# Second attention layer of a graph network on one core: the adjacency mask added by TensorE in PSUM instead of by GpSimd in SBUF

## The reference

```python
v = einsum('bnd,hdo->bhno', x, Wv) + bv
q = einsum('bnd,hdo->bhno', x, Wq) + bq
k = einsum('bnd,hdo->bhno', x, Wk) + bk
scores = einsum('bhno,bhmo->bhnm', q, k) / dk
scores = leaky_relu(scores, 0.2)
scores = scores + (-1e10 * (1.0 - edge_index))[:, None, :, :]
prop = softmax(scores, axis=-1)
feats = einsum('bhnm,bhmo->bhno', prop, v)
out = leaky_relu(mean(feats, axis=1), 0.2)
```

## Time and profile before

| | us |
|---|---|
| median of 3 runs (3578.19 to 3587.32) | 3586.21 |
| the profiled execution | 3591.9 |
| its span | 3590.1 |
| TensorE matmul busy, of the span | 3095.4 |
| VectorE busy | 3037.3 |
| ScalarE busy | 2911.2 |
| GpSimd busy | 1018.2 |

### The profile page before, as it was taken

One profiled execution on the slowest core, in us unless ns is written; L12 is line 12 of the kernel. 1 busy time (PEld: TensorE's weight loads), 2 busy tenths in 40 slices (PEclk: granted clock), 3 DMA queues, 4 the chain that ended last, 5 costly groups with the idle time before them and its releaser, 6 DMA issues. The chain is left out here.

```text
span 3590.1 us, 77844 instructions
## 1 busy us (share of the span) xinstructions
PE 3095.4 (86%) x30972; PEld 1700.4 (47%) x30972; DVE 3037.3 (85%) x4709; ACT 2911.2 (81%) x3505; POOL 1018.2 (28%) x629
## 2 busy tenths in 40 slices
PE   7987998999999969888898898888988988978886
PEld 5664666666666633333333333333333333336665
DVE  6666787778777779999999999999999999975665
ACT  4665777777777759999999999999999999975665
POOL 4433665556656600000000100000001010005764
PEclk9998999999999979999999999999999999987777
DMA  7630000000000000000000000000000000002211
GB/s 244 213 132 20 21 21 21 19 19 21 20 19 21 18 10 10 10 10 10 7 13 10 10 10 10 10 10 7 13 10 10 10 7 13 10 5 69 57 56 33
DMA packets 68394, 111.44 MB, mean 31 GB/s; under 512 B 26452, under 2 KB 26582, under 8 KB 68054
## 3 DMA queue, kind: packets, MB, share of 16 engines
q1 hardware_dynamic: 68054, 106.69, 9.7%
HBM read 86.61 MB, written 18.87 MB: 29 GB/s over the span
## 5 line engine op out<-in xcount | busy, mean ns | idle before, releaser
L1029 ACT ACTIVATE l_scalar_ring<-l_w,l_r 128x1024 f32<-128x1024 f32 x1632 | 1713.1, 1142 | 37.9 <-DVE l_values L1075 27.6
L1143 DVE TENSOR_SCALAR l_vector_ring<-l_w_code,l_r_code 128x2048 f32<-128x2048 f32 x1232 | 1588.9, 1354 | 3.5 <-issue 0.6
L966 PE MATMUL scores<-l_scalar_ring,l_signs 128*32 128x512 f32 x6528 | 794.1, 605 | 90.7 <-ACT l_scalar_ring L1029 90.4
L976 PE MATMUL scores<-l_vector_ring,l_signs_code 128*32 128x512 f16 x9856 | 673.3, 395 | 136.7 <-DVE l_vector_ring L1143 135.8
L242 ACT COPY probs_t<-turned 128x512 f32<-128x512 f32 x576 | 324.3, 586 | 484.9 <-PE turned L201 484.8
L450 POOL TENSOR_TENSOR l_masked<-l_relu,mask 128x1024 f32<-128x1024 f32 x256 | 545.7, 2132 | 419.8 <-ACT l_relu L607 384.6
L976 PEld LDWEIGHTS scores<-l_vector_ring,l_signs_code 128*32 128x32 bf16 x9856 | 243.3, 96 | 589.8 <-DVE l_vector_ring L1143 300.8
L201 PE MATMUL turned<-ident,l_probs 128*128 128x128 f32 x3072 | 440.6, 289 | 12.1 <-issue 7.9
L269 ACT ACTIVATE l_probs<-l_logits,negmax 128x1024 f32<-128x1024 f32 x384 | 443.5, 1155 | 7.6 <-DVE negmax L260 7.6
L966 PEld LDWEIGHTS scores<-l_scalar_ring,l_signs 128*32 128x32 f32 x6528 | 201.0, 110 | 469.6 <-issue 262.9
L260 DVE CUSTOM_DVE_ANT_0 l_logits<-scores,l_masked,l_bound 128x1024 f32<-128x1024 f32 x256 | 328.3, 1282 | 107.3 <-POOL l_masked L450 73.1
(11 more groups left out here) (240 smaller groups left out, 3129.4 us busy)
## 6 DMA issues: line engine op xcount, KB each, us to landing
mask<-masks_kept SPq DMA_DIRECT2D x192, 256.0 KB, 2.6
l_adj<-adj SPq DMA_DIRECT2D x64, 512.0 KB, 5.7
masks_kept<-l_mask_ring SPq DMA_DIRECT2D x64, 256.0 KB, 4.7
x_res<-x SPq DMA_DIRECT2D x8, 256.0 KB, 5.1
out<-x_res SPq DMA_DIRECT2D x8, 256.0 KB, 2.7
l_h<-l_h SPq DMA_DIRECT2D x8, 128.0 KB, 2.9
l_kl<-l_dh SPq DMA_DIRECT2D x32, 2.0 KB, 1.8
l_kl<-l_dl SPq DMA_DIRECT2D x32, 2.0 KB, 1.8
```

Source lines behind the costliest of these rows:

```text
L966: last = nc.tensor.matmul(s.scores[g * ROWS:(g + 1) * ROWS, buf, half, :], signs[:, window], scalar_ring[:, at % SCALAR_RING, g, halves[ha ...
L976: last = nc.tensor.matmul(s.scores[g * ROWS:(g + 1) * ROWS, buf, half, :], signs_code[:, par, g % 2, window], parts(vector_ring[:, at % VE ...
L1029: last = nc.scalar.activation(scalar_ring[:, at % SCALAR_RING, g, :], w[:, par, :], ACT.Relu, bias=r[:, par, column:column + 1])
L1143: last = nc.vector.tensor_scalar(vector_ring[:, at % VECTOR_RING, g:g + 2, :], w_code[:, par, :, :], r_code[:, par, 0, column:column + 1], ...
```

## The change

In the second layer `score` gets one more multiplication for each half: the bf16 mask as the moving operand against a bf16 identity, as the first of the three that add up in the bank. TensorE, not GpSimd, waits for the mask's transfer. The relu of ScalarE now reads masked scores (it gives zero where the mask is), and its buffer is free once VectorE has taken the unit's logits. VectorE's instruction adds the masked scores in PSUM and the relu, and waits for the relu. GpSimd's addition and the tile `masked` go; GpSimd keeps the layer norm's parts. The transfer of the next mask waits for the scores that read the old one. The bf16 identity is one small copy at the layer's start.

```diff
-        sems = make_sems(nc, ctx, layer, ["x_in0", "x_in1", "x_in", "relu_ready", "masked_ready", "bound_ready",
+        sems = make_sems(nc, ctx, layer, ["x_in0", "x_in1", "x_in", "relu_ready", "bound_ready",
...
-        masked = sb("masked", [P, 2, N], F32) if leaky else None
+        ident16 = sb("ident16", [P, P], BF16) if leaky else None
...
                 for m in range(B * NB):
-                    wait(sp, sems["masked_ready"], (m - 1) * H)
+                    wait(sp, sems["scores_ready"], (m - 1) * H)
                     load_mask(sp, s, sems, m, m % 2)
...
-            def mask_relu(pair, i, n, u):
-
-                if n % H == 0:
-                    g.wait_ge(sems[f"mask_in{i}"], 16 * pair + 16)
-                g.wait_ge(sems["relu_ready"], u + 1)
-                wait(g, sems["logits_ready"], STARTS + u - 1)
-                nc.gpsimd.tensor_tensor(masked[:, n % 2, :], relu4[:, n % 2, :], s.mask[:, i, :], ALU.add
-                                        ).then_inc(sems["masked_ready"], 1)
...
-                    if leaky and not (last_graph and n + 3 >= U):
-                        i = ((n + 3) // H) % NB
-                        mask_relu((b + (n + 3) // U) * (NB // 2) + i // 2, i % 2, n + 3, b * U + n + 3)
...
-            if leaky:
-                for u in range(3):
-                    mask_relu(0, 0, u, u)
-            else:
+            if not leaky:
                 layer_norm_centre(g, s, sems, 0, 0)
...
+                if leaky and h == 0:
+                    pe.wait_ge(sems[f"mask_in{i % 2}"], 16 * (b * (NB // 2) + i // 2) + 16)
                 rows = slice(i * P, (i + 1) * P)
                 for half in range(2):
                     cols = slice(half * BANK, (half + 1) * BANK)
                     out = s.scores[:, n % 2, half, :]
-                    nc.tensor.matmul(out, h2[:, par, rows], kh[:, par, h, cols], start=True, stop=False)
+                    if leaky:
+                        nc.tensor.matmul(out, ident16[:], s.mask[:, i % 2, cols], start=True, stop=False)
+                    nc.tensor.matmul(out, h2[:, par, rows], kh[:, par, h, cols], start=not leaky, stop=False)
                     last = nc.tensor.matmul(out, h1[:, par, rows], kl[:, par, h, cols], start=False, stop=True)
...
             def relu(n, u):
                 a.wait_ge(sems["scores_ready"], u + 1)
-                wait(a, sems["masked_ready"], u - 1)
+                wait(a, sems["logits_ready"], STARTS + u - 1)
...
                 if leaky:
-                    v.wait_ge(sems["masked_ready"], u + 1)
-                    masked_max(v, s, sems, scores[n % 2], n % 4, neg_scale, logits[:, n % 2, :], masked[:, n % 2, :])
+                    v.wait_ge(sems["relu_ready"], u + 1)
+                    masked_max(v, s, sems, scores[n % 2], n % 4, neg_scale, logits[:, n % 2, :], relu4[:, n % 2, :])
...
             if leaky:
+                nc.vector.tensor_copy(ident16[:], s.ident[:])
```

## The result

| | before | changed |
|---|---|---|
| median, 20 runs each, us | 3586.77 | 3596.84 |
| lowest to highest | 3576.71 to 3595.68 | 3586.20 to 3611.15 |
| profiled execution / its span | 3591.9 / 3590.1 | 3597.7 / 3595.9 |

The ratio is 1.0028, with a 95% interval of 1.0016 to 1.0040: 10 us slower, between 6 and 14. The forecast was +16.5, on a slightly lower median. The measured time lies in the forecast's range, but the +16.5 itself lies above the interval.

The account below looks back on a forecast made before the run. TensorE's pace was taken as the bound: 830.3 us of own work plus 127.8 of stalls. Masks 109.7 plus remaining stalls 35.1 less 127.8 gave +17.0, with -0.6 ahead about +16.5: 3602.7 us, range 3583 to 3634.

Parts of the forecast that it names:

- The masks' price: TensorE's two extra 512-column multiplications a unit: 0.43 us a pair, rounds of 3.52 or 3.95, 109.7 us over 255 rounds.
- Where they come to lie: At line 234 TensorE finds its operand ready with 0.5 us to spare and sets the pace in ordinary rounds, at 3.52.
- Line 138 and line 159: VectorE's mean and variance lines: without GpSimd's addition, 138 falls from 1.63 to 0.17 us, 159 from 0.57 to about 0.17.
- the list of the starts: Stalls left at graph starts: 3.0 us for four ordinary ones, 0.7 plus 3.0 for graph 6, 3.2 for the layer's first two rounds.
- Round 9: TensorE's wait for the copy behind round 8's variance: 1.0 us left in each of 8 graphs, 8.0 in all.
- Rounds behind a fill: Where `finish` has the last head: take-out 0.17 late, copy 0.12 late, five rounds a graph in seven graphs, 4.2 us.
- The loop's turns: The turns to graphs 2 and 4, with slower work at the lower clock behind them: 6.5 us each, 13.0 in all.
- Ahead of the layer's first transposes: GpSimd's 2.13 us leaves the first unit's path, masks at the lower clock, 0.86 a unit, enter it: -0.6 us.
- list of stalls: TensorE stalls expected to remain from VectorE's order and the program's flow: 35.1 us in sum, against 127.8 before.
- rival A: More stalls go than listed; if a third of the 35.1 goes, the layer moves by +5, about 3591 us; chance 0.27.
- Rival B: VectorE stays late, masks come on top of stalls that don't go: layer +63, 3649 us; chance 0.15.
- Rival C: At `score`, masks cost less than the fp16 pairs; at 0.215 us a pair the layer moves by -38, 3548; chance 0.08.

Follow-up runs that it names:

- addition aside: The changed kernel with a same-sized GpSimd addition for every unit, on its own tiles, for which nobody waits: 3619.6 us, ratio to before 1.0108.
- both additions: The kernel before with TensorE's mask multiplications added and GpSimd's addition kept: 3641.5 us, ratio to before 1.0155.

## Why the prediction was right

- **The masks' price.** Foreseen: 0.43 us a unit, from a fill of the same shape. Measured: 3.51 and 3.95 a round, and 3.94 with two pairs. The number of pairs was off: 253 in the stretch and not 255, as its last two rounds score no unit. That is 0.9 of the 17.
- **Where they come to lie.** Foreseen: TensorE becomes the pace and VectorE's operand is there in time. Shown by the waits at line 234, 46.6 before and 8.6 after, and by stalls of 31.1 where 35.1 were listed. The two runs without masks and with both give the whole square: GpSimd's addition made 50 us of stalls alone and 30.5 beside the masks, and the masks' 108.8 us cost 62.0 without GpSimd's addition and 42.6 with it. Each edit hides part of the other, and their sum is +12.1.
- **Line 138 and line 159.** Foreseen: 0.17 without GpSimd. Measured: 0.17 in all sixteen. The addition aside shows that this is sharing and no wait for a result: 22.4 of the 30.5 us come back with it. I had looked only at the two lines, and a graph's start gained more than listed. The mis-sized term is the list of the starts: for the layer's first two rounds 3.2 were left in the prediction, and 3.35 + 4.39 is no longer than TensorE's own work with masks, 3.52 + 4.38; for graph 6 there were 3.0 for a first pass, and its rounds 0 and 1 are 3.32 and 4.49, a stall of 0.1. Together some 6 us too many. The four ordinary starts came to 3.4 where 3.0 were listed.
- **Round 9.** Foreseen: a stall of 1.0 in eight graphs, 8.0. Measured: 4.86 - 3.95 = 0.9 in six graphs and 0.75 in the last two, 6.9.
- **Rounds behind a fill.** Foreseen: 4.2 us in all. In a graph of the loop round 5 has 0.37 too much, rounds 13, 17, 21, 25 and 29 have 0.19 and round 7 has 0.09, so 1.4 a graph; round 21 has 0.35 more in graphs 0, 2 and 4. That is some 10 in all. This is the term on the other side, 6 too small; it cancelled the starts.
- **The loop's turns.** Foreseen: 13.0. Measured: rounds 31 of 8.08 and 7.69 and the rounds 0 behind them of 4.85 and 4.99, together 11.5 over 3.52 each.
- **Ahead of the layer's first transposes.** Foreseen: -0.6. Measured: 308.77 - 310.13 = -1.4.

So the mechanism held, and the forecast of +16.5 for a measured +10 is the difference of small terms. That the list of stalls came out so close, 35.1 against 31.1, is partly luck: three of its terms (the starts, round 9 and the turns) were too large by 8.6 us together, and one, the rounds behind a fill, too small by 6. What rival A named did happen: the start of graph 6 was quicker and the lower clock didn't come. It did not carry the time because the rounds behind a fill took as much back. The upper end of the range, 3634, is half of B's size above the forecast and not above the kernel before, as its wording suggests; nothing else hangs on it. Rival B is out: TensorE's waits at line 234 fell, and from 320 to 1250 us its wait at line 212 for `finish` of 18.1 us is gone from the view. Rival C is out by the masks issued twice.

What stays open: whether there is more behind the time of the run with both additions (some 45 us over the changed kernel, give or take 14) than the 30.5 of its stretch. Its fourth layer was longer in the profile, which it was by chance in other runs too; no run was made for it. An earlier start of the mask's transfer could not matter, as no wait for it shows, and was not tried.

## What to carry to other kernels

Before work is moved to the engine with the tightest queue, count that engine's own work in a round from its starts and take the rest as a budget of stalls: here 128 us of stalls had to pay for 109 of masks, and what counted was which of the stalls would really go. An operation that is "hidden" on GpSimd can still cost time through the VectorE instructions that run beside it; look for small ones that last as long as GpSimd does, and put them where nobody waits behind them. If two engines can each do a job and both limits are near, split it: with the norm parts moved, a quarter of the columns on TensorE was 0.4% faster than all on GpSimd and 1.0% faster than all on TensorE.

## What the hardware showed that I had not expected

TensorE's clock at a graph's start. In the kernel before TensorE waited 1.69 us for the copy behind line 138 in graph 6, and the round after ran at the lower level of its clock (1.2 of 2.4 GHz) for a while; in the changed kernel, in the same place, it did not. The same stretch behind that wait, before and then changed (length, busy time of PE, PEld, DVE, ACT and POOL, the granted clock as a share of 2.4 GHz, DMA):

```profile
1045.00:1049.00 4.00, 3.89 (x24) 2.49 (x26) 2.21 (x6) 1.21 (x3) 0.53 (x1) 0.57 0.19 70
```

```profile
1053.80:1057.80 4.00, 4.00 (x46) 2.86 (x44) 2.43 (x7) 3.21 (x5) 1.99 (x2) 1.00 0.08 28
```

The granted clock was 0.57 before and 1.00 after, and round 1 of that graph went from 7.54 to 4.49 us; in the layer's first graph it went from 8.20 to 4.39. Graphs 1, 3 and 5 had a stall of the same kind before, kept the full clock, and took 5.97 in round 1, so the lower clock was worth some 1.6 us in graph 6. This is where the starts of graphs 0 and 6 gained more than I had listed.

A wait of this length can lower the clock, but doesn't always. With the addition aside TensorE waited 1.64 us for the copy of line 249 in round 9 of every graph (1.65 in the last). Behind that wait the clock fell in graph 0 and in no other. Here are graph 0 and then graph 1, with the same columns:

```profile
346.61:350.61 4.00, 4.00 (x18) 1.76 (x20) 2.02 (x5) 1.45 (x2) 0.35 (x1) 0.57 0.01 2
473.41:477.41 4.00, 4.00 (x36) 2.70 (x37) 2.96 (x7) 1.60 (x2) 1.29 (x1) 1.00 0.01 2
```

Nor did it fall behind the waits of 1.75 in graphs 1, 3 and 5 of the kernel before. In the changed kernel TensorE's longest wait at line 234 is 0.65 us, and the clock fell behind none of them. So the shorter waits fit the higher clock; what decides between two waits of the same length stays open.
